# Global attention of a four-layer network: scores formed a second time with the keys on the partitions, instead of turning the probabilities

## What is computed

```python
gate = jax.nn.sigmoid(z)[:, :, None]
s = xf * gate
theta = jnp.einsum('oc,ncl->nol', theta_w, s) + theta_b[None, :, None]
phi = jnp.einsum('oc,ncl->nol', phi_w, s) + phi_b[None, :, None]
g = jnp.einsum('oc,ncl->nol', g_w, s) + g_b[None, :, None]
attn = jax.nn.softmax(jnp.einsum('nci,ncj->nij', theta, phi), axis=-1)
nl = jnp.einsum('ncj,nij->nci', g, attn)
nl = jnp.einsum('oc,ncl->nol', out_w, nl) + out_b[None, :, None]
out = s + nl
```

## Time and profile before

| | |
|---|---|
| median of 3 runs | 7107.38 us (7102.32 to 7118.62) |
| the profiled execution, own time | 7109.38 us |
| its span, first to last instruction | 7107.3 us |
| mean granted TensorE clock | 0.969 of 2.4 GHz |
| `softmax2`, first score matmul to first matmul of `project_out2`, each image | 355.9 us |

### The profile page before, as it was taken

How to read it: one execution, slowest core, us unless ns; L and a number is a source line. 1 busy time by engine, 2 the same in 40 slices (tenths; PEclk the granted TensorE clock), 3 DMA queues, 4 the chain that set the end, 5 groups by cost and what they waited for, 6 DMA issues and landing times. The chain is left out here.

```text
span 7107.3 us, 136255 instructions
## 1 busy us (share of the span) xinstructions
PE 6218.9 (88%) x38014; PEld 4169.0 (59%) x38014; DVE 6060.1 (85%) x9428; ACT 5703.7 (80%) x8984; POOL 5398.8 (76%) x3379
## 2 busy tenths in 40 slices
PE   6777899996888888888888888888888888888888
PEld 4545676763555555555555555555555555555555
DVE  5444444444999999999999999999999999999998
ACT  5372332333999999999999999999999999999998
POOL 4351000003999999999999999999999999999997
PEclk8786999997999999999999999999999999999999
DMA  3221000002000000000000000100000000000000
GB/s 98 67 69 44 1 0 0 0 0 65 11 1 1 1 1 1 1 11 1 1 1 1 1 1 2 29 1 1 1 1 1 1 2 1 4 4 4 4 4 6
DMA packets 110735, 79.83 MB, mean 11 GB/s; under 512 B 68490, under 2 KB 108290, under 8 KB 109826
## 3 DMA queue, kind: packets, MB, share of 16 engines
q1 hardware_dynamic: 107306, 77.71, 3.8%
q10 hardware_dynamic: 3288, 0.33, 0.0%
HBM read 48.70 MB, written 22.86 MB: 10 GB/s over the span
## 5 line engine op out<-in xcount | busy, mean ns | idle before, releaser
L1594 POOL TENSOR_TENSOR a_s<-a_s,a_v 128x784 f32<-128x784 f32 x1568 | 2910.7, 1856 | 310.0 <-ACT a_s L1804 298.1
L1630 PE MATMUL a_right_sides<-a_s,diag_d 128*128 128x392 f32 x6272 | 2288.9, 508 | 14.7 <-POOL a_s L1594 1.0
L1630 PEld LDWEIGHTS a_right_sides<-a_s,diag_d 128*128 128x128 f32 x6272 | 1134.3, 191 | 1064.7 <-POOL a_s L1594 345.3
L1725 DVE SCALAR_TENSOR_TENSOR a_kan<-a_s,spline_c,a_kan 128x784 f32<-128x784 f32 x1568 | 1622.2, 1035 | 51.4 <-DVE a_kan L1714 0.9
L1587 POOL TENSOR_TENSOR a_inner<-a_inner,a_x 128x784 f32<-128x784 f32 x784 | 1458.9, 1861 | 0.0
L1804 ACT ACTIVATE a_s<-a_v 128x784 f32<-128x784 f32 x1568 | 1335.2, 852 | 4.6
L1795 ACT ACTIVATE a_v<-a_a 128x784 f32<-128x784 f32 x1568 | 1335.1, 852 | 0.3
L1652 PEld LDWEIGHTS a_weighed<-a_V,a_probT 128*128 128x128 f32 x9800 | 1232.4, 192 | 162.2
L1652 PE MATMUL a_weighed<-a_V,a_probT 128*128 128x65 f32 x9800 | 1223.5, 269 | 0.0
L1642 PE MATMUL a_turned<-ident,a_prob 128*128 128x128 f32 x4900 | 794.0, 280 | 325.8 <-ACT a_probT L1812 323.7
L1617 PE MATMUL a_scores<-a_K,a_q 32*64 32x392 f32 x6272 | 703.8, 515 | 273.0 <-DVE a_kan L1707 241.8
(11 more groups left out here) (198 smaller groups left out, 5293.8 us busy)
## 6 DMA issues: line engine op xcount, KB each, us to landing
rows<-bias_rows_dram SPq DMA_DIRECT2D x112, 91.0 KB
ve<-v_dram SPq DMA_DIRECT2D x98, 104.0 KB
X<-in_x_dram SPq DMA_DIRECT2D x4, 1568.0 KB, 13.8
xn<-kt SPq DMA_DIRECT2D x56, 112.0 KB, 2.2
v_dram<-vt SPq DMA_DIRECT2D x56, 112.0 KB, 2.0
a_q<-q_dram SPq DMA_DIRECT2D x392, 16.0 KB, 2.0
mask<-in_window_mask_dram SPq DMA_DIRECT2D x56, 98.0 KB, 1.9
a_V<-v_dram SPq DMA_DIRECT2D x4, 812.5 KB, 8.6
```

The costliest lines, as they stand in the source:

```text
L1594: eng.tensor_tensor(s, s, v, ALU.mult).then_inc(cubed, 1)
L1630: mm = eng.matmul(up[:, j, 0:SUB], steps[i][:, :], cubes[g][:, SUB * j:SUB * (j + 1)], start=(i == 0), stop=(i == 1))
L1725: eng.scalar_tensor_tensor(F, banked((s1, s2)[j][g][:, :]), c[:, 3 + j:4 + j], F, ALU.mult, ALU.add).then_inc(left_added, 1)
```

## The change

`softmax2` is written anew. It walks over the queries in 7 blocks of 448 (`QB`). For each block the scores are formed twice. By query: 4 tiles of 112 queries times 7 stretches of 448 keys, in 16 groups of one or two matmuls; DVE reads them only for the maximum, and what it writes (`scratch`) is not used. The four columns of maxima are put on a diagonal (`shares`) and spread over all partitions with a matrix of ones (`spread_max`), and ACT copies them to `limit`. By key: for each of the 25 key tiles PE forms 128 keys x 448 queries (`by_key`), DVE subtracts the limit (`take_limit`), ACT exponentiates in place, POOL adds the result to `acc`, and four steps later PE multiplies it with g (`values`). The transposes, their copies, the copy of the queries and the accumulated sums of ACT are gone. At a block's end PE spreads the sums of `acc` (`spread_sums`), DVE inverts 128x448 of them (`invert`) and multiplies the output by that (`divide`). The score groups of the next block are issued between the steps 4 to 19 of the present one. The loop is written out; nothing is rolled.

The removed body is the one printed above; here are the added lines.

```diff
@@ -993,8 +993,6 @@
-PAIR2 = 2 * P
-TURNS2 = L // PAIR2 + 1
...
@@ -1127,151 +1125,180 @@
 
 def softmax2(nc, m, b, theta, phi, gT, nl):
 
...
+    QB, QT2 = CHUNK, TILE
+    BLOCKS, GROUPS = CHUNKS, 16
+    LAG, RING = 4, 6
+    STEPS = BLOCKS * KEY_TILES2
     first_key = lambda k: min(P * k, L - P)
...
+    keys_of = lambda g: [c for c in (2 * g, 2 * g + 1) if c < CHUNKS]
     with ExitStack() as st:
         sem = st.enter_context(signals(nc, f"a2_{b}"))
         sb = lambda name, shape: st.enter_context(nc.sbuf_tensor(f"a2_{name}_{b}", shape, F32))
         ps = lambda name, shape: st.enter_context(nc.psum_tensor(f"a2_{name}_{b}", shape, F32))
...
+        scratch = [sb(f"scratch{r}", [QT2, 2, QB]) for r in range(2)]
+        gmax = [sb(f"gmax{r}", [QT2, 4, 4]) for r in range(2)]
+        rmax = [sb(f"rmax{r}", [QT2, 4]) for r in range(2)]
+        share = sb("share", [QT2, 4, QT2])
         ones = sb("ones", [P, P])
...
+        limit = [sb(f"limit{r}", [P, QB]) for r in range(2)]
+        probT = [sb(f"probT{r}", [P, QB]) for r in range(RING)]
+        acc = [sb(f"acc{r}", [P, QB]) for r in range(2)]
+        inv = sb("inv", [P, QB])
+        scp = [ps(f"scores{r}", [QT2, 2, 512]) for r in range(2)]
+        tp = [ps(f"by_key{r}", [P, 512]) for r in range(2)]
+        op = ps("op", [P, 512])
+        spread = ps("spread", [P, 512])
+
+        ones_set, s_made, s_maxed, max_step, share_made, max_spread, limit_kept, t_made, d_taken, exp_done, weighed, acc_done, sums_made, inverted, o_placed = (
+            sem(n) for n in ("ones_set", "s_made", "s_maxed", "max_step", "share_made", "max_spread", "limit_kept", "t_made", "d_taken", "exp_done", "weighed", "acc_done", "sums_made", "inverted", "o_placed"))
+
+        def ahead(s, at):
+            j, k = s // KEY_TILES2, s % KEY_TILES2
+            return j + 1 if k == at and j + 1 < BLOCKS else None
+
+        def behind(s, at):
+            j, k = s // KEY_TILES2 - 1, s % KEY_TILES2
+            return j if k == at and j >= 0 else None
+
+        def group(s):
+            j, k = s // KEY_TILES2 + 1, s % KEY_TILES2 - LAG
+            return GROUPS * j + k if j < BLOCKS and 0 <= k < GROUPS else None
 
         with nc.Block() as block:
             @block.gpsimd
             def _(pool):
...
+                pool.memset(ones[:, :], 1.0).then_inc(ones_set, 1)
+                for n in range(STEPS):
+                    j, k = n // KEY_TILES2, n % KEY_TILES2
+                    low = 0 if k < KEY_TILES2 - 1 else P - TAIL2
+                    pool.wait_ge(exp_done, n + 1)
+                    if n:
+                        pool.wait_ge(acc_done, n)
+                    if k == 0:
+                        if j >= 2:
+                            pool.wait_ge(sums_made, j - 1)
+                        pool.tensor_copy(acc[j % 2][:, :], probT[n % RING][:, :]).then_inc(acc_done, 1)
                     else:
...
+                        pool.tensor_tensor(acc[j % 2][low:P, :], acc[j % 2][low:P, :], probT[n % RING][low:P, :], ALU.add).then_inc(acc_done, 1)
 
             @block.tensor
             def _(pe):
...
+                def scores(a):
+                    j, t, g = a // GROUPS, a % GROUPS // 4, a % 4
+                    at = QB * j + QT2 * t
+                    if a >= 2:
+                        pe.wait_ge(s_maxed, a - 1)
+                    for i, c in enumerate(keys_of(g)):
+                        mm = pe.matmul(scp[a % 2][:, i, 0:QB], theta[:, at:at + QT2], phi[:, QB * c:QB * (c + 1)], start=True, stop=True)
+                    mm.then_inc(s_made, 1)
+
+                def spread_max(j):
+                    pe.wait_ge(share_made, j + 1)
+                    if j >= 2:
+                        pe.wait_ge(inverted, j - 1)
+                    pe.matmul(spread[:, 0:QB], ones[0:QT2, :], share[:, :, :].rearrange("p t q -> p (t q)"), start=True, stop=True).then_inc(max_spread, 1)
+
+                def by_key(n):
+                    j, k = n // KEY_TILES2, n % KEY_TILES2
+                    if n >= 2:
+                        pe.wait_ge(d_taken, n - 1)
+                    pe.matmul(tp[n % 2][:, 0:QB], phi[:, first_key(k):first_key(k) + P], theta[:, QB * j:QB * (j + 1)], start=True, stop=True).then_inc(t_made, 1)
+
+                def values(n):
+                    j, k = n // KEY_TILES2, n % KEY_TILES2
+                    pe.wait_ge(exp_done, n + 1)
+                    if k == 0 and j:
+                        pe.wait_ge(o_placed, j)
+                    pe.matmul(op[:, 0:QB], gT[:, k, :], probT[n % RING][:, :], start=(k == 0), stop=(k == KEY_TILES2 - 1)).then_inc(weighed, 1)
+
+                def spread_sums(j):
+                    pe.wait_ge(acc_done, KEY_TILES2 * (j + 1))
+                    pe.wait_ge(limit_kept, min(j + 2, BLOCKS))
+                    pe.matmul(spread[:, 0:QB], ones[:, :], acc[j % 2][:, :], start=True, stop=True).then_inc(sums_made, 1)
+
                 pe.wait_ge(ones_set, 1)
...
+                for a in range(GROUPS):
+                    scores(a)
+                spread_max(0)
+                for s in range(STEPS + LAG):
+                    if s < STEPS:
+                        by_key(s)
+                    if group(s) is not None:
+                        scores(group(s))
+                    if ahead(s, LAG + GROUPS + 1) is not None:
+                        spread_max(ahead(s, LAG + GROUPS + 1))
+                    if behind(s, 2) is not None:
+                        spread_sums(behind(s, 2))
+                    if s >= LAG:
+                        values(s - LAG)
 
             @block.vector
             def _(dve):
...
+                def row_max(a):
+                    j, t, g = a // GROUPS, a % GROUPS // 4, a % 4
+                    n = len(keys_of(g))
+                    dve.wait_ge(s_made, a + 1)
+                    dve.tensor_scalar(scratch[a % 2][:, 0:n, :], scp[a % 2][:, 0:n, 0:QB], 1.0, None, ALU.mult, ALU.max,
+                                      accum_out=gmax[j % 2][:, t, g:g + 1]).then_inc(s_maxed, 1)
+
+                def shares(j):
+                    dve.wait_ge(s_maxed, GROUPS * (j + 1))
+                    dve.tensor_reduce(rmax[j % 2][:, :], gmax[j % 2][:, :, :], AX.X, ALU.max).then_inc(max_step, 1)
+                    dve.wait_ge(max_step, j + 1)
+                    if j:
+                        dve.wait_ge(max_spread, j)
+                    dve.tensor_tensor(share[:, :, :], m.ident[0:QT2, 0:QT2].unsqueeze(1).to_broadcast([QT2, 4, QT2]),
+                                      rmax[j % 2][:, :].unsqueeze(2).to_broadcast([QT2, 4, QT2]), ALU.mult).then_inc(share_made, 1)
+
+                def take_limit(n):
+                    j, k = n // KEY_TILES2, n % KEY_TILES2
+                    dve.wait_ge(t_made, n + 1)
+                    if n >= RING:
+                        dve.wait_ge(weighed, n - RING + 1)
+                        dve.wait_ge(acc_done, n - RING + 1)
+                    if k == 0:
+                        dve.wait_ge(limit_kept, j + 1)
+                    dve.tensor_tensor(probT[n % RING][:, :], tp[n % 2][:, 0:QB], limit[j % 2][:, :], ALU.subtract).then_inc(d_taken, 1)
+
+                def invert(j):
+                    dve.wait_ge(sums_made, j + 1)
+                    if j:
+                        dve.wait_ge(o_placed, j)
+                    dve.reciprocal(inv[:, :], spread[:, 0:QB]).then_inc(inverted, 1)
+
+                def divide(j):
+                    dve.wait_ge(inverted, j + 1)
+                    dve.wait_ge(weighed, KEY_TILES2 * (j + 1))
+                    dve.tensor_tensor(nl[:, QB * j:QB * (j + 1)], op[:, 0:QB], inv[:, :], ALU.mult).then_inc(o_placed, 1)
+
+                for a in range(GROUPS):
+                    row_max(a)
+                shares(0)
+                for s in range(STEPS + LAG):
+                    if s < STEPS:
+                        take_limit(s)
+                    if group(s) is not None:
+                        row_max(group(s))
+                    if ahead(s, LAG + GROUPS) is not None:
+                        shares(ahead(s, LAG + GROUPS))
+                    if behind(s, 2) is not None:
+                        invert(behind(s, 2))
+                    if behind(s, LAG - 1) is not None:
+                        divide(behind(s, LAG - 1))
+                dve.wait_ge(o_placed, BLOCKS)
 
             @block.scalar
             def _(act):
...
+                def keep_limit(j):
+                    act.wait_ge(max_spread, j + 1)
+                    act.copy(limit[j % 2][:, :], spread[:, 0:QB]).then_inc(limit_kept, 1)
+
+                keep_limit(0)
+                for s in range(STEPS):
+                    act.wait_ge(d_taken, s + 1)
+                    act.activation(probT[s % RING][:, :], probT[s % RING][:, :], ACT.Exp).then_inc(exp_done, 1)
+                    if ahead(s, LAG + GROUPS + 1) is not None:
+                        keep_limit(ahead(s, LAG + GROUPS + 1))
```

(31 more changed lines are left out.)

22 lines of the change are left out of this document (removed).

## The result

The changed kernel takes 7268.7 us (median, 7265.3 to 7271.8) where the kernel before took 7105.2 on the same chip: ratio 1.0226, interval 1.0209 to 1.0244. The forecast was 7256 with 7238 to 7300.

What follows compares the result with a forecast made beforehand. PE's streamed columns bound the softmax stage: 420.3 us of passes plus 9.8 of waits make 430.1 against 355.9, +74.2 per batch, +148.4 for two. From 7109.4 this gives 7257.8, less 2.0 for the median: 7256, range 7238 to 7300.

Steps and rivals of the forecast that it cites:

- The bound: Softmax stage, PE: 160 passes of 448 columns a block at 0.3753 us, 60.05 us; 7 blocks make 420.3 us per batch.
- The edges: Places where PE still waits in the softmax stage, at block starts and ends: sum 9.8 us per batch.
- (f): Before the first score: the copy of the queries on POOL no longer stands there, -0.4 us per batch.
- (a): Start, first block's score groups: PE waits 0.7 us for the buffer of the group before, three times, 2.1 us.
- (b): First block, before the spread of the maximum: PE waits 2.4 us, then 0.2 for limit copy and first subtraction, 2.6.
- (c): 6 later blocks: share product queues behind by_key(20)'s subtraction on DVE, so PE waits 0.4 us each, 2.4 us.
- (d): Last block, no next scores: the last exp and add reach spread_sums after three values, PE waits 0.55 us.
- (e): End of the stage: 0.2 us to the division, 0.62 for it, 1.64 to project_out2, 2.5 us.
- An idle stretch of 2.4 us costs no clock: PE's waits in the softmax stage: claimed full pace afterwards, as project_out2's 28 passes took 10.76 us after 2.29 idle.
- The reciprocal: invert, 128x448 on DVE: taken as 1.5 us, free up to 2.9; upper bounds 3.9 and 5.3; block-edges rival chance 0.15.
- POOL: Rival, adds in the softmax stage: an add with its wait above 1.5 us sets the pace; +39 us, 7295; chance 0.08.
- PE streams faster: Rival, softmax matmul stream: long streams close up below 0.3753 us a pass; at 0.28, 7042 us; chance 0.04.

Runs made afterwards that it cites:

- The four kernels that cut columns: Changed kernel with one score matmul per group, half-width score passes, maximum over 448 keys, or no maximum: 7151.9, 7137.2, 7013.7, 6970.9 us.
- the run without sums: Changed kernel with POOL's adds of 128x448 replaced by a fill of 128x8: 7267.4 us, ratio 1.0235 to the kernel before.

## Why the prediction was right, and what was mis-sized

- **The bound.** PE's columns, as said: 160 passes of 448 columns a block. 420.3 us per image were forecast; at the measured 0.376 a pass it is 1120 x 0.376 = 421.1. The four kernels that cut columns confirm the price: their stages lie 10 to 16 us above their own passes at this price, the changed kernel's 11.7.
- **The edges**, forecast from the first score matmul on: 10.2 (the sum of 9.8 without (f), which lies ahead of it). Measured: (a) 810.10 - 804.14 - 14 x 0.376 = 0.7, three times, 2.1 as forecast. (b) 829.38 - 822.01 - 14 x 0.376 = 2.1, and 0.6 more up to the next scores: 2.7 against 2.6. (c) 0.2 instead of 0.4 in each of the six blocks, 1.3 together, because the share product took 0.62 and not 0.69 and came earlier. (d) 0.5 against 0.55. (e) 3.9 against 2.5. And a term that the sum does not have: 1.3 in front of the last block's values, shown above. Together 11.8, where the stage has 11.7. Term (e) was mis-sized and the last block's wait left out, both because of the reciprocal. They come to 2.7 us, as much as a stage is longer than forecast; the small misses of the others (passes 0.8 more, (c) 1.1 less) nearly cancel.
- **An idle stretch of 2.4 us costs no clock** was read from one wait of 2.29 us. Behind the waits (a) and (b) the clock fell in six of ten stages, 1.45 us each; in the two stages of the changed kernel's first profile, which the sum is held against, it did not.
- **The reciprocal.** I took 1.5 us from the row of 4 columns; it is 2.96, (2.958 - 0.153) / 447 = 6.3 ns a column, between my value and the upper bound of 3.9. In five blocks it costs nothing, by 0.2 us (free up to 2.9 was worked out). That slack was counted alike for all six; the last block has no scores of a next one in it, 1.5 us less, and there PE waits 1.3 us. At the end of each image it is late as well:

```profile
1230.70 1.02 PE L1217 MATMUL a_spread<-a_acc,a_ones 128*128 128x448 f32 x2 [0.27 <-POOL a_acc L1182]
1231.55 1.67 PE L1212 MATMUL a_op<-a_probT,gT 128*128 128x448 f32 x4
1231.76 2.96 DVE L1267 RECIPROCAL a_inv<-a_spread 128x448 f32<-128x448 f32 x1 [2.92 <-PE a_spread L1217]
1234.75 0.62 DVE L1272 TENSOR_TENSOR nl<-a_op,a_inv 128x448 f32<-128x448 f32 x1
```

  PE's values end at about 1231.55 + 4 x 0.376 = 1233.05, and the division could start 0.2 us later; it starts at 1234.75, 1.5 us late. The estimate of 3.9 from the 8 repeats in the Trainium skill, page "VectorE: DVE Perf Modes", section "First, the fixed hardware budget", is nearer than my 1.5, and still above the row, which is about 6 steps of 1.04 ns per column. A row of 4 columns is too narrow to tell such a slope from the fixed part of an instruction.
- **POOL** was sized at 1.15 and measured 1.13, and is hidden but for (d): the run without sums shows it. That rival is out.
- **PE streams faster** is out as well: 0.376 us a pass in the longest stream yet. What the Trainium skill says of sustained pairs ("TensorE: Matmul & The Clock Gate", section "Back-to-back issue gap") brought no closer spacing here for passes of 448 fp32 columns.
- **Nothing beside the stage changes** was what the prediction stood on (what stands before and behind is left as it is), and it is wrong: 13.4 us more behind, some 11 of them from the clock at the end. Forecast 148.4, stages 153.8, measured 159.4 between the profiled executions and 163.5 between the medians. It is luck that the total stayed so near: the first stage began 7.9 us earlier, within the scatter, and took back more than half of it. The cause of the clock there stays open.

## What to carry to other kernels

When an engine is busy 98% of a stage, count what the change makes it stream before anything else: turning the probabilities cost PE one pass of 128 columns per 128x128 square, while a second set of scores costs two, and this decided the case whatever the other engines gave back. The scores by key were the useful half: with the maximum taken from a seventh of the keys, or left out where the range of the scores is known, the same stage fell from 356 to 307 and to 274 us. A long instruction on another engine is free only for as long as the work in front of its reader covers it; shortening that work brings the wait to light, and a larger lag hides most of it again. Check this at the last block too, where the work for the next one is missing.

## What was not expected of the hardware

The reciprocal of 128x448 from PSUM takes 2.96 us, almost five times a subtraction of the same size (0.62). The granted clock stayed at 0.50 for the last 35 us in all ten profiles of the rewritten stage; in both of the kernel before it was 1.00 again from 29 to 5 us before the end, though the lines of the program there are the same.
